# A graph layer's edge loop, its software pipeline shortened by one turn: sums three turns behind the projection, transposes one turn later, edge weights made in the turn of the scores

## The chip, the cores and the metric

The kernel runs on one core of one Trainium2 chip. The metric is the device time of one execution in microseconds; a lower time is better. The time before is the median of three runs.

## The reference, cut to what matters

The layer normalizes 3125 node rows of 256 numbers. An equivariant message passing over 53125 edges, a mixing step over 8 heads and a mixture of 8 experts (2 for each node) follow. The change concerns the edges. For each edge the normalized row of its source node is taken, a row being 64 scalars x0 and 64 vectors x1:

```
r   = edge_vector / |edge_vector|
s0, s1 = x0[src] @ ls0, x1[src] @ ls1
h0, h1 = fctp(s0, s1, r)             # linear maps of s0, of s1 . r, and of s1
sc  = leaky_relu(h0) @ lsc           # scores
act = softmax([sc, 0 x 192])
o0, o1 = fctp(h0, h1, r)
agg = segment_sum(act * [o0, o1], dst)
```

## The kernel before, in words

The edges are sorted by destination and cut into 104 groups of 512 (four tiles of 128). All destinations of one group lie in one window of 40 nodes. Each engine walks the groups in a software pipeline written out by hand: it has its own function `step(i, k)`, and `steps` runs it for some turns ahead (k up to 7), for 8 x 10 turns in a hardware loop, and for the rest unrolled. A step holds work of several groups at different stages. Within an engine the order of the calls is the order of execution. Engines meet through counting semaphores.

What group g goes through, with the turn k in which it happens before the change:

- GpSimd (`gather`, line 556) issues four indirect DMAs which fetch the group's 512 rows into slot g % 10 of a ring `xg`. It waits for the row indices (`stage_idx` on ScalarE, line 1030, made for five groups at once, `AHEAD` = 6 turns ahead) and for `turn_sums`, which says that the slot's last user has been summed.
- VectorE: `products` (L1431) and `dots` (L1439), in turn g - 2: the vector part times r, summed over three components.
- TensorE: `turn_z` (L726) transposes the rows, in turn g - 2; `project` (L741) multiplies with the composed weights in turn g; `turn_hid` (L773) transposes the hidden scalars in turn g + 1; `scores` (L790) in turn g + 2; `scatter` (L813), the window's sums as 12 matmuls with a one-hot matrix as moving data, in turn g + 4.
- ScalarE: `copy_z` (L1087), `outs` (L1129 copies the hidden part out of PSUM, L1130 the outputs), `copy_hid` (L1141), and `exps` (L1115), four exponentials of which each also reads a sum.
- VectorE: `hidden` (L1474, leaky relu) in turn g; `maxima` (L1452) and `messages` (L1528) in turn g + 2; `norms` (L1478), `inverses` (L1497), `hots` (L1462), `weights` (L1504), `vector_weights` (L1516) and `weigh` (L1540, the one-hot matrix times the weights) in turn g + 3; `add` (L1558, the window is added to the sums in SBUF) in turn g + 5.

The VectorE order of a turn before is: products, norms, dots, inverses, hots, add, weights, maxima, vector_weights, hidden, weigh, messages, and in some turns the addition of a mixed row tile (L1605). The 25 row tiles of the head mixing ride along, three in ten turns: a transpose (L769) and a product (L761) on TensorE, a copy (L1104) ahead of the exponentials, and L1605.

TensorE signals twice in a turn. `turn_heads` comes after project, turn_hid and scores; `turn_sums` after scatter and turn_z. In the first turns ScalarE also clears the six planes of the sums (`clear`, L1148), and VectorE finishes the head statistics (`KV_PARTS`). After the loop come the second normalization, the gate and the experts, none of which is touched.

Of the kernel before, what the change touches and what calls it, by code (L numbers as in the profile page):

```python
# [52 lines left out]
def gps_layer_kernel(nc, t, out, dbg=None):  # L53
# [25 lines left out]
    AHEAD = 6  # L79
    HALF = 5  # L80
    FIRST = 8
    TURNS = (G - AHEAD - FIRST - RING) // RING
# [29 lines left out]
    with ExitStack() as ctx:  # L112
# [200 lines left out]
        class GroupSems:  # L313


            def __init__(s, tag, ring):
                s.ring = ring
                s.gathered = [sem(f"{tag}gathered{i}") for i in range(ring)]
                (s.idx, s.prod, s.dot, s.zt_ps, s.zt_sb, s.f_ps, s.o0, s.hid, s.hid_ps, s.hid_t, s.scores, s.neg_top,
                 s.exp, s.hot, s.norm, s.coef, s.eo, s.sel, s.scattered, s.added, s.turn_heads, s.turn_sums) = (  # L320
                    sem(tag + n) for n in ("idx", "prod", "dot", "zt_ps", "zt_sb", "f_ps", "o0", "hid", "hid_ps", "hid_t",
                                           "scores", "neg_top", "exp", "hot", "norm", "coef", "eo", "sel", "scattered",
                                           "added", "turn_heads", "turn_sums"))
# [188 lines left out]
        def _(pool):  # L512
# [130 lines left out]
        def _(pe):  # L643
# [150 lines left out]
            def scatter(i, o):  # L794
# [4 lines left out]
                pe.wait_ge(main.eo, RING * i + o + 1)  # L799
# [5 lines left out]
                return scatter_mm(s, r)  # L805

            def scatter_mm(s, r):

                n = 3 * WIN
                for col, lhs0, coef0 in ((0, 128, 1), (n, 0, 0), (2 * n, 256, 3)):  # L810
# [184 lines left out]
        def _(act):  # L995
# [81 lines left out]
            def copy_z(i, o):  # L1077
                if not group(i, o):
                    return
                s = o % 2  # L1080
                act.wait_ge(main.turn_sums, RING * i + o + 1)
                if not isinstance(i, int) or o >= 2:
                    act.wait_ge(main.turn_heads, RING * i + o - 1)
                copy_z_of(s).then_inc(main.zt_sb, 1)
# [33 lines left out]

            def outs(i, o):
                if not group(i, o):  # L1120
                    return
                act.wait_ge(main.turn_heads, RING * i + o + 1)
# [4 lines left out]
            def outs_of(q, s):  # L1127
                f = f_bank(s).rearrange("p (t f) -> p t f", f=128)
                act.activation(hid[:, s, :, :], f[:, :, M:128], ACT.Copy)  # L1129
                return act.activation(o0[:, q, :, :], f[:, :, 0:M], ACT.Copy)  # L1130

            def copy_hid(i, o):
# [3 lines left out]
                act.wait_ge(main.turn_heads, RING * i + o + 2)  # L1136
# [6 lines left out]
            def clear(i, k):  # L1143

                if isinstance(i, int) and 0 <= k < 6:
                    if k == 4:
                        act.wait_ge(kv_ready, 1)
                    act.activation(agg[:, k, :], zero[:, 0:1].to_broadcast([128, NW]), ACT.Copy).then_inc(agg_zeroed, 1)  # L1148
# [19 lines left out]
            with act.If(far > 0):  # L1168
                with act.Fori(0, G) as g:
# [5 lines left out]
                    act.wait_ge(wide.f_ps, g + 1)  # L1175
                    outs_of(0, 0).then_inc(wide.o0, 1)
# [114 lines left out]
        def _(dve):  # L1291
# [149 lines left out]
            def maxima(i, o):  # L1441
# [4 lines left out]
                dve.wait_ge(main.turn_heads, RING * i + o + 3)  # L1446
# [18 lines left out]
            def hidden(i, o):  # L1465
# [3 lines left out]
                dve.wait_ge(main.o0, RING * i + o + 1)  # L1469
# [11 lines left out]
            def norms(i, o):  # L1481
# [4 lines left out]
                if not isinstance(i, int) or o >= 2:  # L1486
                    dve.wait_ge(main.turn_sums, g + 5)
# [56 lines left out]
            def add(i, o):  # L1544
# [7 lines left out]
                dve.wait_ge(main.turn_sums, g + 7)  # L1552
# [16 lines left out]
            def kv_bias():  # L1569

                own(dve.tensor_tensor(kv_col[:, 1, :], ps3[:, :, 128], kw_col[:, :], ALU.mult))
# [4 lines left out]
            def kv_sums():  # L1576

                dve.wait_ge(rows_ready, 1)
# [14 lines left out]
            KV_PARTS = {-1: kv_weights, 0: kv_bias, 1: kv_sums, 2: kv_whole}  # L1593
# [30 lines left out]
            steps(dve, step, -2, FIRST, TURNS, G + 5)  # L1624
# [269 lines left out]
```

## Time and profile before

| what | value |
|---|---|
| median of 3 runs | 1160.52 us |
| lowest, highest | 1160.38, 1164.48 us |
| span of the profiled execution | 1163.6 us |
| its first products, its last add (L1558) | 79.64 us, 625.00 us |
| TensorE busy | 1056.7 us (91%) |
| VectorE busy | 762.1 us (65%) |
| GpSimd busy | 634.9 us (55%) |
| ScalarE busy | 623.8 us (54%) |

The span of the profiled execution is 3.1 us above the median. No time other than the span is listed for that execution; of the three runs the one of 1164.48 us is the nearest. The edge loop takes 545 us of the span. The shares are means over stages: in the edge loop all four engines are busier than the table says.

### The profile page before, as it was taken

How to read it: one execution, taken by the hardware profiler on the slowest of the kernel's cores; microseconds unless marked ns; L12 is line 12 of the kernel's file. 1: busy time of each engine (PE TensorE's matmuls, PEld its weight loads, DVE VectorE, ACT ScalarE, POOL GpSimd, SP SyncE). 2: the span in 40 equal slices, each digit the busy share in tenths (PEclk: the TensorE clock that was granted, in tenths of full speed). 3: DMA queues.
4: the chain of work that ended last, by engine and by line, in shares of the span. 5: the costliest groups of instructions: out<-in, count | busy, mean ns of one | idle time of the engine just before them, and what ended most of it. 6: DMA issues, size and time to landing. Idle time of an engine off the chain costs nothing.

```text
span 1163.6 us, 27165 instructions
## 1 busy us (share of the span) xinstructions
PE 1056.7 (91%) x8001; PEld 1003.1 (86%) x8002; DVE 762.1 (65%) x1942; ACT 623.8 (54%) x1948; POOL 634.9 (55%) x700
## 2 busy tenths in 40 slices
PE   1377999999999999999998977799999999999993
PEld 1267999999999999999997975699999999999992
DVE  6888999999999999999984658333333333333330
ACT  3329555555555555555554760655555555555550
POOL 2474777777777777777731300444444444444431
PEclk9568999999999999999997989899999999999997
DMA  6532333333333333333320334583222222222224
GB/s 160 160 91 68 111 109 112 103 108 103 109 113 105 110 109 109 109 111 105 105 61 5 106 117 181 177 296 65 36 36 34 38 36 36 36 36 36 35 29 124
DMA packets 47378, 108.51 MB, mean 93 GB/s; under 512 B 13814, under 2 KB 24871, under 8 KB 45160
## 3 DMA queue, kind: packets, MB, share of 16 engines
q0 software_dynamic: 30720, 69.24, 24.2%
q1 hardware_dynamic: 16308, 37.47, 9.9%
q10 hardware_dynamic: 308, 1.28, 0.3%
q8 instruction: 21, 0.34, 0.1%
q14 instruction: 21, 0.17, 0.0%
HBM read 90.88 MB, written 20.27 MB: 96 GB/s over the span
## 4 chain that ended last, share of the span: by engine, by line
PE 44%; issue 15%; DVE 12%; POOL 10%; ACT 9%; DVEq 4%; DMA 4%; SPq 0%; POOLq 0%; ACTq 0%
PE ps L961 17%; PE ps L975 16%; POOL xg L556 10%; ACT e L1115 5%; DMA xg<-xn_rows,idx_st 3%; DVEq L1551 2%; PE ps L813 1%; PE ps L864 1%; DVE neg_top L1452 1%; PE ps L860 1%; PE ps L945 1%; ACT agg L1148 1%; PE ps L889 1%; PE ps L699 1%; PE ps L861 1%
## 5 line engine op out<-in xcount | busy, mean ns | idle before, releaser
L556 POOL DMA_INDIRECT xg<-xn_rows,idx_st x416 | 417.5, 1004 | 170.3 <-issue 124.6
L813 PE MATMUL ps<-sel,xg 128*128 128x120 f32 x2496 | 298.5, 276 | 3.8 <-DVE sel L1540 1.3
L813 PEld LDWEIGHTS ps<-sel,xg 128*128 128x128 f32 x2496 | 286.8, 192 | 10.0 <-issue 9.2
L1266 ACT ACTIVATE ht_sb<-ps,b_cur 128x128 f32<-128x128 f32 x448 | 127.9, 369 | 162.5 <-PE ps L961 162.5
L961 PEld LDWEIGHTS ps<-xst,w_st 128*128 128x128 f32 x1792 | 210.1, 193 | 5.6 <-issue 2.8
L961 PE MATMUL ps<-xst,w_st 128*128 128x128 f32 x1792 | 210.6, 276 | 2.3 <-ACT ht_sb L1266 1.7
L1115 ACT ACTIVATE e<-ps,neg_top 128x65 f32<-128x65 f32 x416 | 125.4, 316 | 161.8 <-DVE neg_top L1452 143.7
L975 PE MATMUL ps<-w_sb,ht_sb 128*128 x896 | 202.8, 379 | 0.8 <-DVE y_sb L1845 0.8
L626 POOL DMA_INDIRECT sum_rows<-y_sb,put_st x56 | 108.4, 1935 | 145.6 <-DVE y_sb L1848 135.4
L975 PEld LDWEIGHTS ps<-w_sb,ht_sb 128*128 128x128 f32 x896 | 166.7, 191 | 21.4 <-issue 1.2
L1845 DVE TENSOR_TENSOR y_sb<-ps,b_bc 128x256 f32<-128x256 f32 x56 | 23.8, 425 | 184.2 <-PE ps L975 184.2
L1256 ACT ACTIVATE w_st<-w_sb 128x1024 f32 x56 | 116.1, 2074 | 33.3 <-DVE etile L1813 32.3
L741 PE MATMUL ps<-w_f,zt 128*128 128x128 f32 x832 | 113.1, 280 | 0.0
L1431 DVE TENSOR_TENSOR prod<-xg,edge_r 128x768 f32<-128x768 f32 x104 | 99.3, 955 | 11.5 <-DMA xg<-xn_rows,idx_st 8.1
L741 PEld LDWEIGHTS ps<-w_f,zt 128*128 128x128 f32 x832 | 104.0, 196 | 0.6
L1540 DVE TENSOR_TENSOR sel<-hot,ps 128x800 f32<-128x800 f32 x104 | 102.2, 982 | 0.3
L1439 DVE TENSOR_REDUCE xg<-prod 128x256 f32<-128x768 f32 x104 | 99.0, 952 | 0.2
L1832 DVE TENSOR_SCALAR w_st<-w_sb 128x1024 f32 x56 | 61.6, 1100 | 42.1 <-PE ps L961 39.1
L612 POOL DMA_INDIRECT xs_sb<-expert_in_rows,take_st x56 | 61.0, 1089 | 48.5 <-POOL take_st L608 48.5
L1115 ACT ACTIVATION_READ_ACCUMULATOR e<-ps,neg_top 128x1 f32 x416 | 85.7, 206 | 0.0
L726 PE MATMUL ps<-ident,xg 128*128 128x128 f32 x416 | 66.3, 283 | 11.2 <-DVE xg L1439 8.8
L1087 ACT ACTIVATE zt<-ps 128x512 f32<-128x512 f32 x104 | 63.5, 611 | 12.4 <-PE ps L726 12.4
(271 smaller groups left out, 1363.1 us busy)
## 6 DMA issues: line engine op xcount, KB each, us to landing
w_sb<-in_L_ffn_W SPq DMA_DIRECT2D x16, 1024.0 KB, 6.8
xg<-xn_rows,idx_st POOLq DMA_INDIRECT x416
x_sb<-in_x SPq DMA_DIRECT2D x5, 560.0 KB
xn_rows<-xn_sb SPq DMA_DIRECT2D x5, 560.0 KB
xn_t<-xn_rows SPq DMA_DIRECT2D x25, 112.0 KB
expert_in_rows<-xf_sb SPq DMA_DIRECT2D x12, 224.0 KB
sum_rows<-x_sb SPq DMA_DIRECT2D x12, 224.0 KB
out<-sum_rows SPq DMA_DIRECT2D x3, 560.0 KB
```

The lines of the kernel that those rows point to most:

```text
L556: pool.indirect_dma_start(xg[:, s, tt, M:M + D], None, xn_dram, bass.IndirectOffsetOnAxis(ap=idx_st[:, s, tt:tt + 1], axis=0)).then_inc(ma ...
L626: pool.indirect_dma_start(sum_dram, bass.IndirectOffsetOnAxis(ap=put_st[:, s:s + 1], axis=0), y_sb[:, s, :], None, compute_op=ALU.add).the ...
L741: mm = pe.matmul(f_bank(s)[:, tt * 128:(tt + 1) * 128], zt[:, s, tt * 128:(tt + 1) * 128], w_f[:, :], start=True, stop=True)
L813: mm = pe.matmul(ps3[:, s, col:col + n], xg[:, r, tt, lhs0:lhs0 + 128], sel[:, s, lo:lo + n], start=(tt == 0), stop=(tt == TG - 1))
L961: mm = pe.matmul(h_of(c), w1_st[:, s, kc, c, :], xst[:, s, kc, :], start=(kc == 0), stop=(kc == 1))
L975: mm = pe.matmul(ps1[:, 1, 0:D], ht_sb[:, o % 2, c, :], w2_sb[:, bass.ds(e, 1), c, :].rearrange("p e d -> p (e d)"), start=(c == 0), stop= ...
L1115: ins = act.activation(e0[:, s, tt, :], score_ps(s)[:, tt * (M + 1):(tt + 1) * (M + 1)], ACT.Exp, bias=neg_top[:, s, tt:tt + 1], accum_out ...
L1256: act.activation(w1_st[:, o % 2, 1, :, :], w1_columns(e, 1), ACT.Copy).then_inc(w1_half1, 1)
L1266: ins = act.activation(ht_sb[:, o % 2, c, :], h_of(c), ACT.Gelu, bias=b1_cur[:, o % 2, c:c + 1])
L1431: return dve.tensor_tensor(prod[:, :, :, :], xg[:, s, :, 128:320].rearrange("p t (u m) -> p t u m", m=3), r, ALU.mult)
L1439: dve.tensor_reduce(xg[:, o % RING, :, 0:M], prod[:, :, :, :], AX.X, ALU.add).then_inc(main.dot, 1)
L1540: return dve.tensor_tensor(sel[:, s, 0:TG * 5 * WIN].rearrange("p (t k w) -> p t k w", t=TG, k=5), hot[:, s, :, :].unsqueeze(2).to_broadca ...
```

## The change

The transposes `turn_z` of a group move from turn g - 2 to turn g - 1 and from the second part of TensorE's turn to the end of the first. The sums move from turn g + 4 to g + 3 and are issued as two sets: the rows' sums, which need only `sel`, and then the messages' sums, which need `eo` too. The VectorE parts that make the weights move from turn g + 3 to g + 2, the turn of the maxima, and `add` from g + 5 to g + 4. VectorE's order in a turn becomes: maxima, hidden, products, norms, inverses, hots, weights, dots, vector_weights, add, weigh, messages. `outs` is divided: the copy of the hidden part comes first in ScalarE's turn and has a semaphore of its own, the copy of the outputs comes last. The clears of the six planes are distributed 2, 2, 0, 1, 1 over turns -1 to 3, where they were one a turn from -1 to 4. The indices are staged 7 turns ahead. The pipeline is started one turn later on TensorE and ends one turn earlier.

```diff
-    AHEAD = 6
+    AHEAD = 7
...
-    TURNS = (G - AHEAD - FIRST - RING) // RING
+    TURNS = (G - AHEAD - FIRST - HALF) // RING
...
-                staged, free = count(pool, RING * i + o + 1), count(pool, RING * i + o - RING + 7)
+                staged, free = count(pool, RING * i + o + 1), count(pool, RING * i + o - RING + 1)
...
-                pe.wait_ge(main.eo, RING * i + o + 1)
                 pe.wait_ge(main.sel, RING * i + o + 1)
...
-                return scatter_mm(s, r)
-
-            def scatter_mm(s, r):
+                scatter_mm(s, r, SUMS_OF_ROWS)
+                pe.wait_ge(main.eo, RING * i + o + 1)
+                return scatter_mm(s, r, SUMS_OF_MESSAGES)
+
+            SUMS_OF_ROWS = ((0, 128, 1), (3 * WIN, 0, 0))
+            SUMS_OF_MESSAGES = ((6 * WIN, 256, 3),)
...
-                ends_with(main.turn_heads, project(i, k), turn_hid(i, k - 1), scores(i, k - 2))
-                ends_with(main.turn_sums, scatter(i, k - 4), turn_z(i, k + 2))
-
-            steps(pe, step, -2, FIRST, TURNS, G + 4)
+                ends_with(main.turn_heads, project(i, k), turn_hid(i, k - 1), scores(i, k - 2), turn_z(i, k + 1))
+                ends_with(main.turn_sums, scatter(i, k - 3))
+
+            steps(pe, step, -1, FIRST, TURNS, G + 3)
...
+            def out_hidden(i, o):
+                if not group(i, o):
+                    return
+                act.wait_ge(main.turn_heads, RING * i + o + 2)
+                out_hidden_of(o % 2).then_inc(main.hid_raw, 1)
...
+            CLEARED_AT = {-1: (0, 1), 0: (2, 3), 2: (4,), 3: (5,)}
...
             def step(i, k):
+                out_hidden(i, k)
+                exps(i, k - 2)
                 copy_z(i, k + 1)
+                copy_hid(i, k - 1)
                 outs(i, k)
-                copy_hid(i, k - 1)
-                exps(i, k - 2)
                 if k + AHEAD >= RING and (k + AHEAD) % HALF == 0:
                     stage_idx(i, k + AHEAD)
-                clear(i, k + 1)
+                for plane in CLEARED_AT.get(k, ()):
+                    clear(plane)
...
-            KV_PARTS = {-1: kv_weights, 0: kv_bias, 1: kv_sums, 2: kv_whole}
+            KV_PARTS = {-2: kv_weights, -1: kv_bias, 0: kv_sums, 1: kv_whole}
...
             def step(i, k):
+                maxima(i, k - 2)
+                hidden(i, k)
                 products(i, k + 2)
-                norms(i, k - 3)
+                norms(i, k - 2)
+                inverses(i, k - 2)
+                hots(i, k - 2)
+                weights(i, k - 2)
                 dots(i, k + 2)
-                inverses(i, k - 3)
-                hots(i, k - 3)
-                add(i, k - 5)
-                weights(i, k - 3)
-                maxima(i, k - 2)
-                vector_weights(i, k - 3)
-                hidden(i, k)
-                weigh(i, k - 3)
+                vector_weights(i, k - 2)
+                add(i, k - 4)
+                weigh(i, k - 2)
                 messages(i, k - 2)
                 add_mixed(mix_tile(i, k - 3))
...
-            steps(dve, step, -2, FIRST, TURNS, G + 5)
+            steps(dve, step, -2, FIRST, TURNS, G + 4)
```

## Rows read from the trace of the kernel before

**Rows 1.** Busy us by engine in one stretch: PE, PEld, DVE, ACT, POOL, clock, DMA
```profile
300.00:400.00 100.00, 99.20 (x852) 95.94 (x851) 92.28 (x237) 55.43 (x249) 76.23 (x79) 1.00 0.38 109
```

**Rows 2.** Timeline of POOL: start, duration, instruction, idle before and its releaser
```profile
109.68 1.37 POOL L556 DMA_INDIRECT xg<-xn_rows,idx_st  x1 [11.33 <-ACT idx_st L1030]
...
595.44 0.95 POOL L556 DMA_INDIRECT xg<-xn_rows,idx_st  x1 [0.30 <-issue]
```

**Rows 3.** Timeline of DVE: the products of groups 20, 30 and 103
```profile
175.17 0.96 DVE L1431 TENSOR_TENSOR prod<-xg,edge_r 128x768 f32<-128x768 f32 x1 [0.24 <-issue]
...
225.09 0.96 DVE L1431 TENSOR_TENSOR prod<-xg,edge_r 128x768 f32<-128x768 f32 x1 [0.18 <-issue]
...
599.80 0.96 DVE L1431 TENSOR_TENSOR prod<-xg,edge_r 128x768 f32<-128x768 f32 x1 [1.78 <-DMA xg<-xn_rows,idx_st]
```

**Rows 4.** Timeline of DVE and ACT in one plain turn
```profile
117.86 0.42 DVE L1452 TENSOR_REDUCE neg_top<-ps 128x4 f32<-128x260 f32 x1
...
118.28 0.42 DVE L1474 SCALAR_TENSOR_TENSOR hid<-hid 128x256 f32<-128x256 f32 x1
118.32 0.32 ACT L1115 ACTIVATE e<-ps,neg_top 128x65 f32<-128x65 f32 x1 [2.13 <-DVE neg_top L1452]
118.61 0.98 DVE L1540 TENSOR_TENSOR sel<-hot,ps 128x800 f32<-128x800 f32 x1
...
119.72 0.43 DVE L1528 TENSOR_TENSOR xg<-e,o 128x256 f32<-128x256 f32 x1
...
120.06 0.95 DVE L1431 TENSOR_TENSOR prod<-xg,edge_r 128x768 f32<-128x768 f32 x1
...
120.93 0.16 DVE L1478 SCALAR_TENSOR_TENSOR norm<-e,exp_sum 128x4 f32<-128x4 f32 x1
121.05 0.95 DVE L1439 TENSOR_REDUCE xg<-prod 128x256 f32<-128x768 f32 x1
...
122.61 0.42 DVE L1452 TENSOR_REDUCE neg_top<-ps 128x4 f32<-128x260 f32 x1
```

**Rows 5.** Timeline of PE in the same turn
```profile
117.70 0.60 PE L726 MATMUL ps<-ident,xg 128*128 128x128 f32 x4
...
118.14 1.06 PE L741 MATMUL ps<-w_f,zt 128*128 128x128 f32 x8
...
119.03 0.38 PE L773 MATMUL ps<-ident,hid 128*128 128x128 f32 x2
...
119.70 2.90 PE L813 MATMUL ps<-sel,xg 128*128 128x120 f32 x24
```

**Rows 6.** Timeline of the work on mixed row tiles: ACT, DVE, PE
```profile
308.87 0.38 ACT L1104 ACTIVATE xn_tt<-ps 128x250 f32<-128x250 f32 x1 [2.43 <-DVE neg_top L1452]
...
310.88 0.42 DVE L1605 TENSOR_TENSOR x_sb<-x_sb,mixed 125x256 f32 x1
...
314.65 0.51 PEld L761 LDWEIGHTS ps<-kv,xn_tt 128*125 128x125 f32 x4
```

**Rows 7.** Timeline of DVE in the last turns, without products and dots
```profile
619.07 0.16 DVE L1478 SCALAR_TENSOR_TENSOR norm<-e,exp_sum 128x4 f32<-128x4 f32 x1
619.26 0.19 DVE L1497 RECIPROCAL ps<-norm 128x4 f32<-128x4 f32 x1
...
620.07 0.41 DVE L1558 TENSOR_TENSOR agg<-agg,ps 128x240 f32 x1 [0.41 <-issue]
...
625.00 0.41 DVE L1558 TENSOR_TENSOR agg<-agg,ps 128x240 f32 x1 [2.83 <-PE ps L813]
```

**Rows 8.** Timeline of ACT and DVE in the first turns
```profile
82.87 0.60 ACT L1087 ACTIVATE zt<-ps 128x512 f32<-128x512 f32 x1 [12.39 <-PE ps L726]
83.37 2.83 ACT L1148 ACTIVATE agg<-zero 128x3168 f32<-128x3168 f32 x1
...
95.33 1.28 ACT L1115 ACT_TABLE_LOAD   x1
...
113.13 0.42 DVE L1452 TENSOR_REDUCE neg_top<-ps 128x4 f32<-128x260 f32 x1
```

More of the change, by code:

```diff
@@ L318, in __init__ @@
                 s.gathered = [sem(f"{tag}gathered{i}") for i in range(ring)]
-                (s.idx, s.prod, s.dot, s.zt_ps, s.zt_sb, s.f_ps, s.o0, s.hid, s.hid_ps, s.hid_t, s.scores, s.neg_top,
+                (s.idx, s.prod, s.dot, s.zt_ps, s.zt_sb, s.f_ps, s.o0, s.hid_raw, s.hid, s.hid_ps, s.hid_t, s.scores, s.neg_top,
                  s.exp, s.hot, s.norm, s.coef, s.eo, s.sel, s.scattered, s.added, s.turn_heads, s.turn_sums) = (
-                    sem(tag + n) for n in ("idx", "prod", "dot", "zt_ps", "zt_sb", "f_ps", "o0", "hid", "hid_ps", "hid_t",
+                    sem(tag + n) for n in ("idx", "prod", "dot", "zt_ps", "zt_sb", "f_ps", "o0", "hid_raw", "hid", "hid_ps", "hid_t",
                                            "scores", "neg_top", "exp", "hot", "norm", "coef", "eo", "sel", "scattered",
@@ L804, in scatter, with scatter_mm @@
                     pe.wait_ge(kv_ready, 1)
-                return scatter_mm(s, r)
-            def scatter_mm(s, r):
+                scatter_mm(s, r, SUMS_OF_ROWS)
[3 more added lines that the diff above has]
+            SUMS_OF_MESSAGES = ((6 * WIN, 256, 3),)
+            def scatter_mm(s, r, sets=SUMS_OF_ROWS + SUMS_OF_MESSAGES):
                 n = 3 * WIN
-                for col, lhs0, coef0 in ((0, 128, 1), (n, 0, 0), (2 * n, 256, 3)):
+                for col, lhs0, coef0 in sets:
                     for tt in range(TG):
@@ L1080, in copy_z @@
                 s = o % 2
-                act.wait_ge(main.turn_sums, RING * i + o + 1)
-                if not isinstance(i, int) or o >= 2:
-                    act.wait_ge(main.turn_heads, RING * i + o - 1)
+                act.wait_ge(main.turn_heads, RING * i + o + 1)
                 copy_z_of(s).then_inc(main.zt_sb, 1)
@@ L1117, in exps_of, with out_hidden_of @@
                 return ins
+            def out_hidden(i, o):
[3 more added lines that the diff above has]
+                out_hidden_of(o % 2).then_inc(main.hid_raw, 1)
+            def out_hidden_of(s):
+                f = f_bank(s).rearrange("p (t f) -> p t f", f=128)
+                return act.activation(hid[:, s, :, :], f[:, :, M:128], ACT.Copy)
             def outs(i, o):
@@ L1121, in outs @@
                     return
-                act.wait_ge(main.turn_heads, RING * i + o + 1)
                 if not isinstance(i, int) or o >= 5:
@@ L1128, in outs_of @@
                 f = f_bank(s).rearrange("p (t f) -> p t f", f=128)
-                act.activation(hid[:, s, :, :], f[:, :, M:128], ACT.Copy)
                 return act.activation(o0[:, q, :, :], f[:, :, 0:M], ACT.Copy)
@@ L1135, in copy_hid @@
                 s = o % 2
-                act.wait_ge(main.turn_heads, RING * i + o + 2)
+                act.wait_ge(main.turn_heads, RING * i + o + 3)
                 copy_mixed(mix_tile(i, o - 1))
@@ L1141, in copy_hid_of, with clear @@
                 return act.activation(hid_t[:, s, :, :].rearrange("p c e -> p (c e)"), ps1[:, 1, 0:TG // 2 * 128], ACT.Copy)
[L1143 to L1148, printed above, removed]
+            CLEARED_AT = {-1: (0, 1), 0: (2, 3), 2: (4,), 3: (5,)}
+            def clear(plane):
+                if plane == 4:
+                    act.wait_ge(kv_ready, 1)
+                act.activation(agg[:, plane, :], zero[:, 0:1].to_broadcast([128, NW]), ACT.Copy).then_inc(agg_zeroed, 1)
             act.wait_ge(xn_written, 16 * 2 * NB)
@@ L1175, in _ @@
                     act.wait_ge(wide.f_ps, g + 1)
+                    out_hidden_of(0)
                     outs_of(0, 0).then_inc(wide.o0, 1)
@@ L1445, in maxima @@
                 s = o % 2
-                dve.wait_ge(main.turn_heads, RING * i + o + 3)
+                dve.wait_ge(main.turn_heads, RING * i + o + 4)
                 if not isinstance(i, int) or o >= 2:
@@ L1468, in hidden @@
                     return
-                dve.wait_ge(main.o0, RING * i + o + 1)
+                dve.wait_ge(main.hid_raw, RING * i + o + 1)
                 hidden_of(o % 2).then_inc(main.hid, 1)
@@ L1486, in norms @@
                 if not isinstance(i, int) or o >= 2:
-                    dve.wait_ge(main.turn_sums, g + 5)
+                    dve.wait_ge(main.turn_sums, g - 1)
                 if not isinstance(i, int) or o >= 1:
@@ L1551, in add @@
                 base = dve.value_load(base_i[0:1, bass.ds(g, 1)], min_val=0, max_val=N)
-                dve.wait_ge(main.turn_sums, g + 7)
+                dve.wait_ge(main.turn_sums, g + 1)
                 if not isinstance(i, int) or o >= 1:
@@ L1569, in kv_bias @@
             def kv_bias():
+                dve.wait_ge(rows_ready, 1)
                 own(dve.tensor_tensor(kv_col[:, 1, :], ps3[:, :, 128], kw_col[:, :], ALU.mult))
@@ L1576, in kv_sums @@
             def kv_sums():
-                dve.wait_ge(rows_ready, 1)
                 for c in (0, 1):
```

## Prediction, made before the changed kernel was run

> **What bounds the kernel now.** I read the windows by stage first. In the middle of the edge loop TensorE is busy 99.2 of 100 us and VectorE 92.3 [rows 1]. GpSimd looks free with 76, but its timeline shows 0.30 us of issue in front of every gather, and 79 gathers make 24 us of that: it is full too. From the first gather of group 10 to the end of the last one it issues 376 gathers without a pause, (595.44 + 0.95 - 109.68) / 94 = 5.18 us a group [rows 2]. Then I followed the products of VectorE. Between groups 20 and 30 they are (225.09 - 175.17) / 10 = 4.99 us apart, faster than GpSimd delivers, and nothing waits for a DMA; the last one waits 1.78 us for its rows [rows 3]. So the loop has two regimes: first it eats the lead of the gathers at 4.99 us a turn, then it walks at GpSimd's pace.
>
> What sets 4.99? One plain turn, from maxima to maxima, is 122.61 - 117.86 = 4.75 us [rows 4]. It is a closed chain: maxima to the first exponential 0.46 (118.32 - 117.86), exponentials to messages 1.40 (119.72 - 118.32), messages to products 0.34, products to norms 0.87, norms to dots 0.12, dots and the small pieces back to maxima 1.56. VectorE is idle in it only before the messages: weigh is out of the way at 118.61 + 0.98 - 0.08 (the overlap of neighbours seen throughout these rows), so 119.51, and messages starts at 119.72. Idle 0.21, work 4.54. TensorE's own work has the same size, 0.44 + 0.89 + 0.67 + 2.74 = 4.74 [rows 5], and its order has slack because each input is made a turn ahead. Turns with mixed tiles are longer, by 0.28 (the copy L1104 stands between maxima and exponentials, 0.38 less the overlap of ScalarE) and by 0.34 (L1605) [rows 6].
>
> **The change, part by part.** No instruction is added or taken away in a full turn; three parts of the price lie elsewhere.
>
> *The turn on VectorE.* Norms now stand in the turn of their own maxima, so the wait for the exponentials stands before norms and not before messages. The latency is the same, 0.46 + 1.40 = 1.86 us after maxima. What covers it: maxima 0.34, hidden 0.33, products 0.87, together 1.54 [rows 4]. Idle 0.32 where 0.21 was. Behind norms the inverses stand at once, and they wait for it. The last turns show that pair bare: 619.26 - 619.07 = 0.19 [rows 7], where norms before gave way after 0.12 [rows 4]: that is 0.08 with rounding. The other dependent pairs have an instruction between them (hots, dots, add), and the read of the window's start in `add` still runs under dots. So a plain turn takes 4.54 + 0.32 + 0.08 = 4.94 us, 0.19 more than now. This is the main term. A wait of products for a DMA of up to 0.3 us is now free, since it falls into the idle time; all that is queued behind norms (dots, weigh, messages and, through them, transposes and sums) is later.
>
> The Trainium skill (VectorE: DVE Perf Modes, "The DRAIN you can't avoid") says that a semaphore after each of a row of chained instructions costs nothing extra. By that rule the 0.08 would fall away and the sum below would be 7.7 us less; the intervals of 0.19 and 0.12 in the rows speak against it here.
>
> *TensorE in the turn.* Sums may start once weigh is done, 0.26 us before the next maxima (0.34 + 0.90 - 0.98), say 0.2 with the hand-over. From there 4.74 us of work end near 4.6 into the turn, and the inputs come earlier: dots end at 1.86 + 0.19 + 0.09 + 0.22 + 0.07 + 0.95 = 3.4, the copy of z by 2.4. TensorE is not the bound in a plain turn; the margin is 0.2 to 0.3. In the turn with a tile's product (loads of 0.51 less overlap, 0.45 [rows 6]) it is late by about 0.22. ScalarE has half its time free and its new order puts nothing ahead of the exponentials that isn't done early.
>
> *GpSimd.* A slot is given back, and indices are staged, a turn earlier in the numbering, so it waits less for either. It issues the same gathers. That buys nothing when VectorE is slower than 5.18 and nothing when GpSimd itself is the pace.
>
> *Mean turn.* From turn 5 to turn 101 there are 96 turns: 96 x 4.94 = 474.2; 25 tiles x 0.62 = 15.5; 25 x 0.22 = 5.5; eight passes of the loop's branch at about 0.25 (the idle 0.24 and 0.18 before products are at such places [rows 3]) = 2.0. Together 497.2, or 5.18 a turn. The same count of ten turns now gives 47.5 + 3 x 0.62 + 0.25 = 49.6 where 49.9 is measured [rows 3], so the method is good to 0.03 a turn, 3 us. Now the stretch from maxima of turn 5 (113.13 [rows 8]) to the products of turn 101 (599.80 [rows 3]) takes 486.7.
>
> *The start.* ScalarE sets it in both kernels. It copies z at 82.87 and then clears [rows 8]. With pairs of clears at 2.73 apart, copies of 0.5 and 0.27, it ends turn -1 at 88.8, turn 0 at 95.3, turn 1's copies at 96.6. VectorE stands in that time at hidden, behind the copy that comes after the clears, and TensorE waits for z. After a projection, scores and a transpose on a partly slow clock, the maxima of turn 2 start at about 99.5. Turn 2 has the table load of 1.28, turn 3 starts near 106.5, and its clear pushes the exponentials of turn 4 by about 0.7: turn 5 starts at 106.5 + 4.9 + 5.6 = 117.0, 3.9 later than now (2 to 6). I take clears at nothing elsewhere: there ScalarE is idle. The first gather of group 10 needs the sums of group 0 and the indices of turn 3, both at about 110, where it is now.
>
> *The end.* There is one turn fewer, but its turns are longer. Without dots the read in `add` isn't covered (inverses to add 0.81 [rows 7], and weights and vector_weights, about 0.4, now stand ahead of it). A turn is 1.86 + 0.19 + 0.09 + 0.22 + 0.19 + 0.70 + 0.31 + 0.90 + 0.34 = 4.8. From maxima of turn 101: 4.9 + 3 x 4.8 + 3.6 to the last weigh + 1.0 + sums 2.9 and hand-over 0.2 = 27.0 us to the last add. Now it is 625.00 - 599.80 = 25.2 from the last products.
>
> *Sum.* 117.0 + 497.2 + 27.0 = 641.2 against 625.0 [rows 7]: +16.2. Everything behind the loop stays. On the profiled span, 1163.6, this is 1180; on the median shown, which is 3.1 lower, 1177.
>
> **Bounds.** The 0.19 a turn is the disputed price. Low end: none of it (then GpSimd is the pace): 0. High end: the margin of TensorE is gone in every turn and the 0.3 comes on top, 4.94 + 0.1: about +10 more. The start is good to 2 us, the end to 2 us. Forecast's own range: 1167 to 1187.
>
> **The rivals.**
>
> *GpSimd stays the pace, no change.* Its last rows would land at about 599.6 as now, if group 10 starts at 110. Turn 101 must then start by about 599, so 96 turns in 482, 5.02 each: my mean turn must be 0.16 too long, nearly the whole difference. For it: in the second half of the loop the machine is already slowed to 5.1 or 5.2 by the gathers, and most of the added latency would vanish in that wait. Against it: 5.18 is counted from the same rows that give 4.99. Time: end 626, 1160 to 1164, with 1161.5. Chance 0.16.
>
> *Faster: the gathers get shorter and the shorter pipeline gives its turn back.* Place: GpSimd. Many gathers take more than the 0.95 of the last one; the mean with issue is 5.18 / 4 = 1.295 where 0.95 + 0.30 = 1.25 is the least. At 1.25 the last rows land 94 x 0.18 = 17 us earlier. To profit, the turn must be below 5.0. With plain turns of 4.94 and the tiles hidden, 96 x 4.95 = 475, the loop ends at 117 + 475 + 27 = 619: -6, 1154.5. It decides from a mean turn of 4.96 downward. For it: longer gathers meet VectorE's dots and products in the timeline, and their places move. Against it: the tiles' 0.28 stands inside the chain. Chance 0.07.
>
> *The wait of the inverses is free.* If they follow norms after 0.12 as dots do now, the turn is 4.86 and the sum 16.2 - 7.7 = +8.5: 1169. For it: the 0.19 is seen only in the last turns [rows 7]. Against it: nothing there but that wait stands between the two. Chance 0.07. This is what the rule of the Trainium skill (VectorE: DVE Perf Modes, "The DRAIN you can't avoid") would make of it.
>
> *TensorE becomes the bound.* The sums wait for weigh, the projection for z, and each wait of TensorE ends too late by 0.15 in every turn: +14 more, 1191. It would show as idle time of TensorE before L813 and L726 in every turn, and as a slow clock at worst. Chance 0.08.
>
> **How the numbers follow.** The forecast +16.2 has 0.62, the four others 0.16, 0.07, 0.07, 0.08. Time 1177. The range leaves out the faster case and part of the case with TensorE late: 1160 to 1190. A change under 0.5% is 5.8 us, about what can't be told from none. Faster 0.07. Same: the case of GpSimd, and a little of the two small ones, 0.18. Slower: the rest, 0.75.
>
> **What would show it.** Right: the waits of products for a DMA are gone or rare through the loop; norms wait about 0.3 for the exponentials in every turn; inverses start 0.19 behind it; plain turns of 4.94; GpSimd has pauses before gathers, released by the sums; turn 5 starts near 117; the last turns are 4.8. Wrong: plain turns under 4.8, or gathers without a pause up to the end as now; or idle time of TensorE above 0.3 in each turn.

## The result, and the profile after

| | before | after |
|---|---|---|
| median, lowest to highest | 1160.86 us, 1160.38 to 1164.48 (4 runs) | 1213.54 us, 1208.97 to 1215.13 (4 runs) |
| span of the profiled execution | 1163.6 us | 1213.4 us |
| last add of the edge loop | 625.00 us | 674.69 us |

The ratio is 1.0437, interval 1.0418 to 1.0456: 4.4% slower. In the profiled executions the whole difference lies in front of the last add (+49.7 us of +49.8), so everything behind the loop is as it was. Taken from maxima to maxima in both kernels, 41.7 us of it lie in the hardware loop (449.7 for 408.1 from turn 8 to turn 88), 4.1 in front of turn 5, 6.1 behind turn 101, and the unrolled turns between are 2.2 shorter.

The four marks of the forecast's sum come from VectorE's timeline of the kernel after: the maxima of turns 5, 8, 88 and 101, and the last add. In this kernel the hardware loop holds turns 8 to 87.

```profile
117.20 0.42 DVE L1466 TENSOR_REDUCE neg_top<-ps 128x4 f32<-128x260 f32 x1
...
132.03 0.43 DVE L1466 TENSOR_REDUCE neg_top<-ps 128x4 f32<-128x260 f32 x1 [0.17 <-PE ps L726]
...
581.77 0.42 DVE L1466 TENSOR_REDUCE neg_top<-ps 128x4 f32<-128x260 f32 x1
...
645.91 0.42 DVE L1466 TENSOR_REDUCE neg_top<-ps 128x4 f32<-128x260 f32 x1
...
674.69 0.41 DVE L1572 TENSOR_TENSOR agg<-agg,ps 128x240 f32 x1 [4.11 <-PE ps L817]
```

| part | forecast | measured | off by |
|---|---|---|---|
| start, to turn 5 | 117.0 | 117.20 | +0.2 |
| turns 5 to 101 | 497.2 | 528.71 | +31.5 |
| turn 101 to the last add | 27.0 | 28.78 | +1.8 |

Start and end came out. The 96 turns took 5.51 each where 5.18 were forecast. The error sits in the hardware loop alone: a pass of ten turns takes (581.77 - 132.03) / 8 = 56.22, where the forecast's terms make 10 x 4.94 + 3 x 0.84 + 0.25 = 52.17. That is 32.4 us too much in eight passes; the 16 turns outside are 0.9 us shorter than forecast (78.97 against 79.8).

The plain turn on VectorE, which answers to [rows 4]: first unrolled (turn 6), then in the hardware loop. Both are of the timeline of after; the value in brackets is idle time and its releaser.

```profile
122.07 0.42 DVE L1466 TENSOR_REDUCE neg_top<-ps 128x4 f32<-128x260 f32 x1
...
122.74 0.95 DVE L1445 TENSOR_TENSOR prod<-xg,edge_r 128x768 f32<-128x768 f32 x1
123.85 0.16 DVE L1492 SCALAR_TENSOR_TENSOR norm<-e,exp_sum 128x4 f32<-128x4 f32 x1 [0.16 <-ACT e L1117]
124.05 0.19 DVE L1511 RECIPROCAL ps<-norm 128x4 f32<-128x4 f32 x1
...
125.30 0.17 DVE L1530 TENSOR_TENSOR ps<-edge_r,ps 128x12 f32<-128x12 f32 x1
125.37 0.41 DVE L1572 TENSOR_TENSOR agg<-agg,ps 128x240 f32 x1
...
126.92 0.42 DVE L1466 TENSOR_REDUCE neg_top<-ps 128x4 f32<-128x260 f32 x1
...
401.47 0.42 DVE L1466 TENSOR_REDUCE neg_top<-ps 128x4 f32<-128x260 f32 x1
...
402.18 0.95 DVE L1445 TENSOR_TENSOR prod<-xg,edge_r 128x768 f32<-128x768 f32 x1
403.35 0.16 DVE L1492 SCALAR_TENSOR_TENSOR norm<-e,exp_sum 128x4 f32<-128x4 f32 x1 [0.22 <-ACT e L1117]
...
404.82 0.17 DVE L1530 TENSOR_TENSOR ps<-edge_r,ps 128x12 f32<-128x12 f32 x1
404.98 0.41 DVE L1572 TENSOR_TENSOR agg<-agg,ps 128x240 f32 x1
...
406.54 0.42 DVE L1466 TENSOR_REDUCE neg_top<-ps 128x4 f32<-128x260 f32 x1
```

Unrolled, the turn is 126.92 - 122.07 = 4.85, close to the 4.94 of the forecast: norms wait for the exponentials, the inverses start 0.20 behind norms. In the loop it is 406.54 - 401.47 = 5.07. The 0.22 more is spread: products to norms 1.17 for 1.11, vector_weights to add 0.16 for 0.07, the rest in steps of 0.01 to 0.03. The loop as such does not cost this. In the kernel before a plain turn takes the same in the loop as unrolled, 4.74 and 4.75 [rows 4]; its timeline of VectorE, a turn in the loop:

```profile
162.84 0.42 DVE L1452 TENSOR_REDUCE neg_top<-ps 128x4 f32<-128x260 f32 x1
...
167.58 0.42 DVE L1452 TENSOR_REDUCE neg_top<-ps 128x4 f32<-128x260 f32 x1
```

The larger part is in the turn of the loop's branch. The chain that ended last, of the same kernel, at one of the passes (start us, us, what; "issue" is time in which the engine waited for nothing that the profile shows):

```profile
355.42 0.42 DVE xg L1542
355.84 0.33 DVE x_sb L1619
356.17 1.68 issue
...
358.05 0.44 DVE neg_top L1466
```

VectorE has done the last work of a pass at 356.17, nothing is missing for the maxima, and they start at 358.05. In the list of waits (us in total, times, longest) of 150 to 600 us that is one line; the others show who waits for whom now.

```profile
POOL xg L556 <- issue: 88.2, 275, 1.6
DVE norm L1492 <- ACT e L1117: 27.5, 80, 0.7
...
PEld ps L817 <- DVE sel L1554: 23.5, 51, 0.7
POOL xg L556 <- ACT idx_st L1034: 16.9, 6, 3.0
POOL xg L556 <- PE ps L817: 16.6, 41, 1.3
...
PE ps L741 <- ACT zt L1089: 15.0, 8, 2.3
DVE neg_top L1466 <- issue: 12.7, 7, 2.0
```

In the kernel before the same places hold 0.24 and 0.18 [rows 3]. The trace also records VectorE's sequencer, which the views leave out: from the loop's branch to its next instruction it takes 2.87 to 3.20 us at the seven branches that are taken, and 0.29 to 0.33 in the kernel before. So the stop stands in front of any wait of the new turn. TensorE is pulled along: with 92.43 us busy in the window where it had 99.20 [rows 1] it is no longer full.

```profile
300.00:400.00 100.00, 92.43 (x772) 88.51 (x772) 87.38 (x219) 51.96 (x230) 71.84 (x70) 0.98 0.35 100
```

Behind the branch it also runs for a while at a lower clock. TensorE's timeline behind the branch of the pass before, whose maxima start at 301.37:

```profile
298.03 0.60 PE L726 MATMUL ps<-ident,xg 128*128 128x128 f32 x4
298.95 2.93 PE L817 MATMUL ps<-sel,xg 128*128 128x120 f32 x24 [0.32 <-DVE sel L1554]
304.07 1.16 PE L741 MATMUL ps<-w_f,zt 128*128 128x128 f32 x8 [2.19 <-ACT zt L1089]
...
305.35 1.07 PE L790 MATMUL ps<-w_sc,hid_t 128*128 128x130 f32 x4
306.22 1.06 PE L726 MATMUL ps<-ident,xg 128*128 128x128 f32 x4
307.07 3.58 PE L817 MATMUL ps<-sel,xg 128*128 128x120 f32 x24
```

After 2.19 us of idle time the same four transposes take 1.06 where they took 0.60: the lower of the clock's two levels, 1.2 for 2.4 GHz, up to somewhere in the sums (3.58 for 2.93). The mean granted clock of the window is 0.98 where it was 1.00.

Taken by place in the pass (mean of eight), the turns are 7.40 (the branch), 5.97 and 5.65 (the two behind it), 5.20, 5.79, 5.08, 5.32, 5.67, 5.07, 5.06. So the 4.05 that a pass is over the forecast divide like this: 10 x (5.07 - 4.94) = 1.3 for the plain turn; 7.40 - 5.07 - 0.34 (the tile's add) - 0.25 = 1.74 for the branch; 0.62 + 0.58 = 1.2 for the two turns behind it; and -0.2 for the mixed tiles, which cost 2.32 a pass instead of 2.52. The sum is 4.04.

What lies in that turn? The lists of DMA queues, page part 3 (packets, MB, share), of before and then of after:

```profile
q14 instruction: 21, 0.17, 0.0%
```

```profile
q14 instruction: 56, 0.46, 0.1%
```

Queue 14 brings instructions, 8192 bytes a packet. In the kernel after, five of its packets go with each branch that is taken, at about -0.2, 1.1, 3.8, 12.8 and 34.9 us from it (medians of seven; one pass has a sixth). In the kernel before, one packet in all lies between the first and the last branch, 174.5 and 532.6 us. The theory for the experiments: VectorE's loop has come to lie so in its instruction stream that its head must be fetched again at each branch.

The Trainium skill (Runtime: NRT & Kernel Launch, "Instruction fetch mechanics") says that an engine's instruction memory is refilled in blocks of 256 instructions, that VectorE's holds two, and that a taken branch to a block not held stalls the engine. The trace agrees in kind, with 1.7 to 2.0 us at each of the seven times that the branch is taken, but its packets are of half such a block, as the next section shows. The prediction had not weighed this.

### The profile page after: what moved, and what is told of

Read it like the earlier page. It is cut to its first block, busy times and chain, and to the rows that moved or that the text cites. A ratio compares the mean times of both kernels' runs of the same rounds, so it can differ in the third digit from the quotient of the medians.

```text
span 1213.4 us, 26957 instructions
## 1 busy us (share of the span) xinstructions
PE 1071.0 (88%) x8001; PEld 1008.3 (83%) x8002; DVE 775.6 (64%) x1942; ACT 630.8 (52%) x1948; POOL 651.7 (54%) x700
## 4 chain that ended last, share of the span: by engine, by line
PE 44%; DVE 22%; ACT 13%; issue 12%; DVEq 5%; DMA 2%; SPq 1%; ACTq 0%; POOL 0%; POOLq 0%
PE ps L965 16%; PE ps L979 16%; ACT e L1117 10%; DVE sel L1554 5%; DVEq L1565 4%; DVE neg_top L1466 3%; DVE xg L1542 2%; PE ps L817 2%; PE ps L868 1%; DVE norm L1492 1%; PE ps L864 1%; DVE xg L1453 1%; PE ps L741 1%; PE ps L949 1%; ACT agg L1159 1%
## 5 line engine op out<-in xcount | busy, mean ns | idle before, releaser
L556 POOL DMA_INDIRECT xg<-xn_rows,idx_st x416 | 431.5, 1037 | 194.1 <-issue 115.6
L817 PE MATMUL ps<-sel,xg 128*128 128x120 f32 x2496 | 308.3, 281 | 20.1 <-DVE sel L1554 18.4
L817 PEld LDWEIGHTS ps<-sel,xg 128*128 128x128 f32 x2496 | 290.6, 194 | 39.5 <-DVE sel L1554 32.8
L1129 ACT ACTIVATE hid<-ps 128x256 f32<-128x256 f32 x104 | 40.0, 385 | 205.7 <-PE ps L726 204.1
L741 PE MATMUL ps<-w_f,zt 128*128 128x128 f32 x832 | 118.7, 287 | 27.0 <-ACT zt L1089 27.0
```

Of the source, the lines that this page charges most:

```text
L741: mm = pe.matmul(f_bank(s)[:, tt * 128:(tt + 1) * 128], zt[:, s, tt * 128:(tt + 1) * 128], w_f[:, :], start=True, stop=True)
L817: mm = pe.matmul(ps3[:, s, col:col + n], xg[:, r, tt, lhs0:lhs0 + 128], sel[:, s, lo:lo + n], start=(tt == 0), stop=(tt == TG - 1))
```

## The experiments

Beside all of these runs but after_lean the kernel before itself took about 1300 us, with pauses of TensorE in the middle of matmuls that wait for nothing; the cause was not found, so these ratios are not comparable with the 1.0437, and I read local intervals first. The last column is the median of the eight intervals from maxima to maxima in which the branch lies; it is 7.64 in the kernel after and 5.45 in the kernel before. A row of such a pause (timeline of TensorE, run after_pad64_timed):

```profile
339.06 1.93 PE L817 MATMUL ps<-sel,xg 128*128 128x120 f32 x15
341.80 0.99 PE L817 MATMUL ps<-sel,xg 128*128 128x120 f32 x5 [0.80 <-issue]
```

| run | us (before beside it) | ratio, interval | q14 packets | branch turn, median |
|---|---|---|---|---|
| after_again | 1331.24 (1305.65) | 1.0193, 1.0125 to 1.0261 | 57 | 7.75 |
| after_pad113 | 1340.94 (1314.35) | one execution | 22 | 5.57 |
| after_pad64 | 1350.33 (1314.35) | one execution | 22 | 5.61 |
| after_pad64_timed | 1332.72 (1301.10) | 1.0193, 1.0126 to 1.0261 | 22 | 5.57 |
| after_pad64_b | 1337.79 (1312.46) | 1.0200, 1.0176 to 1.0224 | 22 | 5.84 |
| after_pad64_c | 1337.49 (1304.74) | 1.0241, 1.0172 to 1.0310 | 22 | 5.68 |
| after_pad64_d | 1351.98 (1314.94) | 1.0249, 1.0176 to 1.0323 | 22 | 5.40 |
| after_pad64_e | 1354.46 (1313.20) | 1.0338, 1.0246 to 1.0430 | 22 | 5.69 |
| before_pad16 | 1316.51 (1314.35) | one execution | 56 | 8.41 |
| before_pad16_timed | 1305.72 (1301.10) | 1.0038, 1.0003 to 1.0074 | 57 | 8.40 |
| before_pad16_b | 1317.91 (1312.46) | 1.0042, 1.0004 to 1.0081 | 57 | 8.14 |
| before_pad16_c | 1319.56 (1313.20) | 1.0042, 1.0004 to 1.0081 | 56 | 8.24 |
| after_add_early | 1334.12 (1314.35) | one execution | 56 | 7.58 |
| after_add_early_timed | 1310.10 (1301.10) | 1.0057, 1.0017 to 1.0097 | 56 | 7.69 |
| after_add_early_b | 1336.15 (1312.46) | 1.0173, 1.0149 to 1.0198 | 56 | 7.44 |
| after_pad64_add | 1335.70 (1312.46) | 1.0192, 1.0156 to 1.0228 | 22 | 5.64 |
| after_all | 1316.89 (1301.10) | 1.0119, 1.0084 to 1.0154 | 22 | 5.71 |
| after_lean | 1217.87 (1163.10) | one execution | 56 | 8.23 |

**VectorE's program moved, after.** 64 (or 113, two lines of that kind) memsets of one element at the head of the program of VectorE; not one instruction of the loop is changed.

```diff
+            for k in range(64):
+                dve.memset(ln_fin[0:1, k // J, k % J:k % J + 1], 0.0)
```

> The changed kernel with 113 memsets of one element put at the head of VectorE's program, where VectorE waits 9 us for its first data; nothing else is touched, and with a fetch unit of 128 instructions the loop then starts at the same place in a unit as in the kernel before. Theory A (place of the program): VectorE's loop body is fetched anew at each pass of the hardware loop because of where it starts, and this costs the 1.9 us of idle in front of the first maxima of each pass. Then the instruction queue has about 21 to 25 packets in place of 56, the turn with the branch is 5.4 in place of 7.7 us, and the time falls by 8 x 2.3 = 18 us or somewhat more, to 1190 to 1197. Theory B (order): the idle belongs to the new order of the turn, whose first instruction after the branch has its wait there. Then nothing changes: 1212 to 1216, 56 packets.

> The same with 64 memsets. Theory A: it is free of the fetches if the harmful starts are a narrow band (then 1190 to 1197), and keeps them if they are half of all starts or more (1212 to 1216). Theory B: 1212 to 1216 in either case.

> The changed kernel with 64 one-element memsets at the head of VectorE's program, timed again in rounds against the kernel before. The instruction queue had 22 packets with it. Theory A (fetches at the loop's branch are 18 us or more of the loss of 52.7): 1188 to 1197, a ratio of 1.025 to 1.032 to the kernel before. Rival (the fetches were seen but hidden, the loss is in the turns): 1208 to 1216, 1.042 to 1.047.

> The changed kernel with 64 one-element memsets at the head of VectorE's program, now where the kernel before takes 1163 us. Its turn with the branch was 5.6 in place of 7.7 us in the earlier profiles. Theory A (the fetches are a cost of the total): 1190 to 1198, ratio 1.024 to 1.032. Rival (as on the disturbed chip, where the total did not move): 1208 to 1216.

> Once more the changed kernel with 64 one-element memsets, alone. Where the kernel before takes 1160 to 1165 us: theory A 1190 to 1198 us (the branch turn 5.6 in place of 7.6, 8 x 2.1 = 17 us), rival 1208 to 1216. Where the kernel before takes 1300, it says nothing new.

> The kernel after with 64 one-element memsets at the head of VectorE's program, which move its hardware loop to another place in the instruction stream. Theory (the loop's fetches of instructions cost about 2 us a pass): packets of q14 fall from 56 to 22, the turn with the branch from 7.6 to 5.6 us, and if the kernel before is at its 1161 us beside it, the total falls by 8 x 2 = 16 us, from 1213 to about 1197, ratio 1.031. Rival (TensorE, busy 92 to 95 us of 100, takes back what VectorE gains): the local turn falls and the total stays at 1210 or over, ratio 1.042 or more.

> After with 64 one-element memsets at the head of VectorE's program. Theory (fetches of instructions cost about 2 us a pass): the turn with the branch at 5.6 instead of 7.6 us and, where the kernel before is at 1161 us beside it, a total of about 1197 us. Rival (TensorE takes it back): the turn falls, the total stays at 1210 or over.

The branch turn of after_pad64_timed on VectorE's timeline: the tile's addition ends a pass, and the maxima of the next start 0.33 behind it, as anywhere.

```profile
357.76 0.41 DVE L1621 TENSOR_TENSOR x_sb<-x_sb,mixed 125x256 f32 x1
358.09 0.42 DVE L1468 TENSOR_REDUCE neg_top<-ps 128x4 f32<-128x260 f32 x1
```

In all seven runs the branch turn falls from 7.7 to 5.4 to 5.8, with 22 packets in place of 56, and from the branch to the sequencer's next instruction it is 0.26 to 0.36 us again. The place of the program decides the fetches, not its content: shown. Where no pause hits them, the branch turn is 5.40 and the two turns behind it are 5.65 and 5.34 (7.40, 5.97 and 5.65 in the kernel after, as means; the 5.97 comes from four passes in which the maxima wait for TensorE's transposes, the other four have 5.67). Together that is 2.00 + 0.32 + 0.31 = 2.63 a pass, 21.0 us in eight. The totals show none of it: the ratios, 1.019 to 1.034, are not under the 1.0193 of the unpadded kernel; the last is above it, with intervals that just touch. With TensorE's pauses the mean turn of the loop is 6.7 to 7.0 in all of these, and its pace is set elsewhere. So the local cost is measured, and its share in the 49.7 us is not.

The changed kernel itself, without any edit, beside a kernel before with the same pauses:

> The changed kernel itself, for the level that the edits of the other runs are to be held against. If the present chip treats both kernels alike, the ratio to the kernel before is 1.044 as in the result (1.042 to 1.046). If the disturbance of TensorE's instruction stream seen in these runs (pauses of 0.5 to 1.2 us in the middle of its matmuls, about every 26 us, in every kernel) covers part of the loss, it is lower, 1.02 to 1.04.

**VectorE's program moved, before.** 16 memsets at the same place.

```diff
+            for k in range(16):
+                dve.memset(ln_fin[0:1, k // J, k % J:k % J + 1], 0.0)
```

> The kernel before with 16 memsets of one element at the head of VectorE's program, which moves its loop to the place (within one instruction) that it has in the changed kernel. Theory A: the fetches appear in the loop, 21 packets of the instruction queue become about 55, and the time rises by 8 x 2 = 16 us, less what the wait for the gathers hides, to 1168 to 1178. Theory B: 1160 to 1165, 21 packets.

> The kernel before with 16 memsets, which brings the fetches (56 packets) into its loop. Theory A: each pass gets about 2 us longer, partly hidden where the gathers are the pace: 4 to 16 us slower than before, ratio 1.004 to 1.014. Rival: no change, 0.998 to 1.003.

> The kernel before with 16 memsets, its loop at the place of the changed kernel's, so with fetches at each pass. Theory A: the branch turn goes from 5.4 to 7.5 or more, 8 x 2 = 16 us, of which the wait for the gathers (whose pace is the bound in the second half) hides a part: 1167 to 1178. Rival (fetches cost nothing in this order of the turn, as little as the 0.4% on the disturbed chip): 1161 to 1165.

> Before with 16 one-element memsets at the head of VectorE's program. Theory: packets of q14 rise from 21 to 56, the turn with the branch from 5.45 to about 8.3 us, and, where the kernel before is at 1161 us beside it, the total rises by 8 x 2.8 = 22 us to about 1183. Rival (the slack of the other turns of a pass covers it): the turn rises, the total stays within 5 us of before.

The mirror image: 56 packets, a branch turn of 8.1 to 8.4 where it was 5.45, and the wait now stands in front of the products, which begin a turn in this kernel. From its list of waits (150 to 670 us), against 1.5 us in 8 waits, longest 0.2, in the kernel before:

```profile
DVE prod L1433 <- issue: 20.6, 7, 3.2
```

So the kernel before was in a good place by at most 16 instructions, and the change moved the loop out of it. The numbers behind it, the sequencer's own instructions included: the body of the loop has 322 instructions before and 320 after, and 252 and 267 of VectorE's stand ahead of it.

By blocks of 256, two of them held (the Trainium skill, the same page and section), all of these runs agree with one unknown offset, as an estimate: the body must start in the first 190 or 192 of a block; if the one before starts at 189 or 190 (178 to 190 without after_lean, whose body of 310 is fetched again too), it falls out with 16 more, the one after (+15) stands from 193 on and is out, and with 64, 90 or 113 more it is in the first quarter of the next block.

The trace speaks for units of half that size. The packets have 8192 bytes and come one at a time, and the last two of a pass are about 21.8 us apart, in which the loop runs 21.8 / (56.2 - 3.0) x 320 = 131 instructions. Units of 128 agree with all runs as well, as an estimate, if a body is fetched again once its end reaches into a fourth unit: before then starts at 61 or 62 of a unit, +16 and after (+15) lie behind the last good place (62 and 64), and with 64, 90 or 113 more the start is at about 12, 37 or 61 and fits. No run decides between the two readings.

The three runs with several executions put the price in the total at 0.4%, about 5 us, where the waits at the branch are 20 to 21. Time that VectorE loses in the kernel before is mostly covered in these runs; in the undisturbed kernel before the gathers of GpSimd have 24% of the chain from 130 to 600 us and their transfers 7%. But TensorE's pauses cover as well in these runs, and the two can't be told apart.

**The idle time in front of norms.** `add` is moved between products and norms, where VectorE waits for the exponentials anyway.

```diff
                 products(i, k + 2)
+                add(i, k - 4)
                 norms(i, k - 2)
...
                 vector_weights(i, k - 2)
-                add(i, k - 4)
                 weigh(i, k - 2)
```

> The changed kernel with VectorE's add moved from behind vector_weights to between products and norms, where VectorE waits for the exponentials. Theory: the idle in front of norms (0.18 to 0.31 us a turn) is a price of making the weights in the turn of the scores. The add (0.32) then fills it, a plain turn falls from 4.86 to about 4.6 outside the loop and from 5.07 to about 4.85 in it, and the time falls by 96 x 0.25 = 24 us to about 1189. Rival: TensorE, whose work is 4.74 us a turn, takes over at once, and the gain is at most 96 x 0.1 = 10 us, 1204. The fetches at the branch stay (no instruction is added).

> The changed kernel with add between products and norms. Theory: the idle time in front of norms is a price of the change, add fills it: 0.2 to 0.3 us a turn, 1184 to 1194. Rival: TensorE with 4.74 us of work a turn takes over, 1200 to 1206.

> The changed kernel with add in front of norms, fetches still in the loop. VectorE's starts add up to about 4.8 us a turn in place of 4.86 outside the loop and 5.07 in it (vector_weights to weigh is 0.27, for it now waits for them). Theory: 80 x 0.25 and a shorter drain, 20 to 25 us less than the changed kernel, 1189 to 1194. Rival (TensorE bound): 1202 to 1208.

> Both edits, the 64 memsets and the early add. If the two prices are independent and the gathers (5.0 to 5.2 us a group) do not take over: the sum of both, 38 to 43 us less than the changed kernel, 1171 to 1176. If the gathers or the mixed tiles' turns take over: 1176 to 1185.

The list of waits, 150 to 680 us: in after_pad64_timed, and then in after_add_early_timed, which ran beside it.

```profile
DVE norm L1494 <- ACT e L1117: 20.2, 63, 0.7
```

```profile
DVE norm L1492 <- ACT e L1117: 2.5, 9, 0.4
```

The idle time is gone and the shortest turns in the loop are 4.91 instead of 5.06. It isn't the 0.2 to 0.3 of the wait, because weigh now stands directly behind vector_weights, whose result it needs: 0.27 between their starts, where the add stood. Once it is 1310.1 beside 1332.7 for the padded kernel (intervals of the ratios apart), once 1336.2 beside 1337.8 (overlapping), with the two edits together at 1335.7; none of them ran beside the changed kernel itself. The gain in the total is not shown.

**The wait instructions in front of norms.** norms waits for three semaphores, of which two (`turn_sums`, `norm`) came long before. Their waits are moved in front of products.

```diff
                 norm_of(o % 2).then_inc(main.norm, 1)
+
+            def norms_free(i, o):
...
+                g = RING * i + o
...
+                norms_free(i, k - 2)
                 products(i, k + 2)
```

> The changed kernel with one edit: norms' waits for the sums and for the norms before it stand ahead of products, so that the wait for the exponentials is on the norms instruction itself. Theory: inside the hardware loop products to norms are 1.21 us (1.11 outside it) because the wait stands in an instruction of its own there, behind register work; with the edit it falls to about 1.11 in the loop too, plain turns from 5.07 to 4.97, the time by 80 x 0.1 = 8 us against the changed kernel. Rival: the 0.1 is the register work itself and stays; the time stays within 3 us. The fetches at the branch stay, 7.6 us for that turn.

> Three edits of the changed kernel together: 90 memsets at the head (no fetches in the loop), add in front of norms, and the waits of norms for the sums and for the norms before it moved ahead of products, so that norms itself waits for the exponentials alone (which should take away most of the 0.1 us that products to norms are longer inside the hardware loop than outside it, 1.21 against 1.11). Theory: the three prices add up, 18 + 24 + 8 = 50 us, and what is left is the pace of the gathers, 5.0 to 5.2 us a group, so the time is that of the kernel before within 5 us: 1156 to 1166. If the prices do not add up (TensorE bound at 4.9 to 5.1 in every turn and a wait for the gathers on top): 1170 to 1180.

Beside after_lean the kernel before took its 1161 us (1163.1). VectorE's timeline: a plain turn of it, and its branch turn.

```profile
345.91 0.95 DVE L1445 TENSOR_TENSOR prod<-xg,edge_r 128x768 f32<-128x768 f32 x1
346.94 0.16 DVE L1492 SCALAR_TENSOR_TENSOR norm<-e,exp_sum 128x4 f32<-128x4 f32 x1
...
355.08 0.42 DVE L1624 TENSOR_TENSOR x_sb<-x_sb,mixed 125x256 f32 x1
358.42 0.43 DVE L1466 TENSOR_REDUCE neg_top<-ps 128x4 f32<-128x260 f32 x1 [2.92 <-issue]
```

Products to norms is 1.03 here, in other plain turns 1.10 or 1.11, instead of 1.17 to 1.21: in this loop two waits that are already fulfilled, with the register operations that belong to them, cost about 0.1 us when they stand behind the one that matters. Plain turns are 5.02 and 4.98. The total is 4 us longer all the same, and VectorE's stop at the branch grew: 20.0 us in seven waits where it was 12.7. The edit took ten instructions out of the body, and the first packet now comes 0.8 us behind the branch instead of 0.2 in front of it. The eight passes took 454.9 us where they took 449.7: the branch turns and the two turns behind them grew by 8.5 (7.86, 6.46 and 5.76 for 7.40, 5.97 and 5.65), and the seven other turns of a pass became shorter by 3.2. So, one execution against one and without TensorE's pauses, all that the stop grew went into the time of the loop.

after_all, with this edit, the early add and 90 memsets, has 1.0119; its branch turn is 5.71. The version nearest to the kernel before was after_add_early_timed with 1.0057 (1.0017 to 1.0097), among the pauses; none reached it.

## Why the prediction was wrong, and where it was right

**Right.** The direction, and a part of the cause: the wait for the exponentials moved in front of norms, and the loop is closed over VectorE. The start (117.20 for 117.0), with the late clears in it. The plain turn, as far as it is unrolled, 4.85 for 4.94: the pair norms and inverses at 0.20 as taken from [rows 7], the idle time 0.24 instead of 0.32 (1.11 from products to norms, less 0.87). The turns that run the pipeline out, 4.86 for 4.8. GpSimd has pauses, released by the sums (41 waits) and the indices, and products wait for no DMA. The mixed tiles, 2.32 a pass for 2.52.

**The step that failed** is the term "eight passes of the loop's branch at about 0.25 = 2.0". I took its price from the kernel before, whose loop lay in a place where its head is not fetched again, and carried it over as if it belonged to the branch. "No instruction is added or taken away in a full turn" left out that 15 more stand ahead of the loop. The branch was 1.74 more in the branch turn itself, and 1.2 more in the two turns behind it, together 2.9 a pass and 23.5 us. By the local intervals of the padded runs the fetches make 2.63 a pass, 21.0 us, with the forecast's 0.25 in it: well placed, the branch turn is 5.40, which is the loop's plain turn and the tile's add (5.07 + 0.34) and nothing for the branch. The other 0.6 a pass, in the two turns behind, is there in the padded runs too, and its cause is open. That the method gave 49.6 for the 49.9 of ten turns before could not show it: those turns are of the same well placed program. (The 486.7 beside the 497.2 ends at the products of turn 101; to its maxima, at 602.34, it is 489.2. The sum does not use it.)

**A term of the wrong size** is the plain turn inside the hardware loop: 5.07 for 4.94, in 80 turns 10.4 us. The forecast took a turn in the loop to be as long as one outside, which holds for the kernel before (4.74 and 4.75) and not here (5.07 and 4.85). The largest parts: 0.09 between vector_weights and add, where the sequencer reads the window's start (the chain from 132 to 582 us has 8.7% on that, DVEq L1565), so the read was not free, and 0.06 in front of norms, which the moved waits of after_lean remove. The end is 1.8 us off; the last sums ran at the lower clock, 4.57 us where the set before took 2.94.

**The rivals.** GpSimd as the pace, and the faster case, fell with the gathers that wait. The free inverses fell: they start 0.20 behind norms in every turn. The Trainium skill (VectorE: DVE Perf Modes, "The DRAIN you can't avoid") says, of a row of copies, that the semaphore costs nothing extra. The trace of this pair doesn't agree, with 0.20 where norms gave way to dots after 0.12 [rows 4]; no run separates the wait from the kind of the second instruction. TensorE as the bound fell too: 92.43 of 100 us busy, with waits for `sel` and `zt`; the few turns in which it is late are those behind the branch.

**Open.** How much of the 49.7 us goes away when VectorE's loop lies well: no padded kernel ran without TensorE's pauses; the bounds are nothing and 21.0 us. For the upper bound speaks after_lean, where the growth of the stop went into the loop in full, and the size of the other paces: with all of it gone a mean turn of the loop would be 5.36, an estimate, against 5.18 for the gathers [rows 2] and 4.74 for TensorE's own work [rows 5]. The kernel would then be at about 1192.5, still above the range. What makes TensorE pause. Why the ratio of this change is 1.019 there and 1.044 here; that a pace set by TensorE's pauses hides VectorE's longer turn is a reading, not shown.

## What to carry to other kernels

When an edit changes the number of instructions ahead of a hardware loop, or in it, look at the instruction queue's packets before and after, and at the "issue" time in front of the first instruction of a pass: a loop body of 320 instructions can be moved into or out of a good place by 16, and some tens of small instructions ahead of it (64, 90 and 113 here) move it back. A price read at a branch in one program is not a price of the branch in the next. If a hardware loop is the stage that counts, take the intervals of a turn from the loop and not from unrolled turns, and expect them to change with the order of the waits, and put waits that are long fulfilled in front of work, not behind the wait that matters.

## What the runs showed of the hardware that was not expected

- VectorE's instructions are fetched again in every pass of a loop when it lies badly: 56 packets of 8 KB against 21, 1.7 to 2.0 us without work at each branch (2.7 to 2.9 with two waits moved, 2.7 to 3.4 in the kernel before moved by 16 instructions). The sequencer stands still for 2.8 to 3.8 us behind the branch, against 0.3.
- The packets have 8192 bytes, and one comes for every 130 instructions or so that the loop runs.
- Behind such a stop TensorE ran at its lower clock as well: after 2.19 us of idle time four transposes took 1.06 us instead of 0.60.
- The same instructions can stand further apart in a hardware loop than unrolled, 5.07 against 4.85 us a turn of 12 instructions on VectorE in the kernel after; in the kernel before, with another order, they do not (4.74 and 4.75).
